# Reading one branch's result early and loading whole 128-partition tiles in the last two stages of a four-layer network

## The reference, cut to what matters

```python
ys = mamba_fwd(xs, spa_...)                     # over all pixels, 64 channels: the pixel mamba
ye = mamba_fwd(xe, spe_...)                     # over 8 tokens of each pixel's channels: the channel mamba
spa = silu(group_norm(ys, spa_gn_w, spa_gn_b, 4)) + x
spe = x + silu(group_norm(ye, spe_gn_w, spe_gn_b, 4))
w = softmax(att_w)
return spa * w[0] + spe * w[1] + x
```

## Time and profile before

| | us |
|---|---|
| median of three runs | 7533.4 |
| profiled execution, its own time | 7550.36 |
| span of that execution, first to last instruction | 7548.5 |
| channel mamba, first to last DMA issue | 5501.7 to 7320.2 |
| merge, first DMA issue to the end of the span | 7326.4 to 7548.5 |

### The profile page before, as it was taken

How to read it: one execution, slowest core, us unless ns; L and a number is a source line. 1 busy time by engine, 2 the same in 40 slices (tenths; PEclk the granted TensorE clock), 3 DMA queues, 4 the chain that set the end, 5 groups by cost and what they waited for, 6 DMA issues and landing times. The chain is left out here.

```text
span 7548.5 us, 120463 instructions
## 1 busy us (share of the span) xinstructions
PE 6575.4 (87%) x36560; PEld 3443.7 (46%) x36560; DVE 5590.7 (74%) x5630; ACT 3977.8 (53%) x6794; POOL 3832.4 (51%) x2716
## 2 busy tenths in 40 slices
PE   8968699999967379687999999999989999999970
PEld 7852233333345134574222222222257777777750
DVE  4653677777712278103999999999979999999974
ACT  4424466666612457103666666666655555555532
POOL 0100122222200300002888888888879999999960
PEclk9989799999978689757999999999989999999985
DMA  2243234334355523533222222222200000000016
GB/s 70 72 169 124 68 99 100 100 99 101 96 127 151 229 81 100 130 86 56 37 37 36 37 37 37 39 39 38 29 16 10 10 10 10 10 10 10 8 40 190
DMA packets 638233, 518.91 MB, mean 69 GB/s; under 512 B 249981, under 2 KB 569251, under 8 KB 629563
## 3 DMA queue, kind: packets, MB, share of 16 engines
q1 hardware_dynamic: 637947, 515.62, 27.9%
HBM read 304.91 MB, written 171.32 MB: 63 GB/s over the span
## 5 line engine op out<-in xcount | busy, mean ns | idle before, releaser
L2582 DVE TENSOR_TENSOR_SCAN spa_hs<-spa_p_d,spa_hs,spa_bx 128x483 f32<-128x483 f32 x1168 | 1370.3, 1223 | 21.1 <-ACT spa_p_d L2495 21.1
L2302 POOL TENSOR_TENSOR spa_hc<-spa_hs,spa_cr 128x966 f32<-128x966 f32 x592 | 1219.0, 2069 | 240.7 <-DVE spa_hs L2582 239.3
L2725 POOL TENSOR_TENSOR spe_hc<-spe_hs,spe_bcu 128x1024 f32<-128x1024 f32 x520 | 1219.7, 2362 | 64.5 <-DVE spe_hs L2937 63.5
L2937 DVE TENSOR_TENSOR_SCAN spe_hs<-spe_p_d,spe_bx 128x1024 f32<-128x1024 f32 x520 | 1161.4, 2275 | 35.0 <-ACT spe_p_d L2885 31.7
L2812 PEld LDWEIGHTS spe_p_y<-spe_idt,spe_hc 128*128 128x128 f32 x8320 | 965.1, 192 | 143.8 <-issue 143.8
L1065 DVE TENSOR_REDUCE attention_nm<-attention_p_s 128x2 f32<-128x640 f32 x1024 | 789.1, 812 | 260.2 <-PE attention_p_s L922 259.1
L2812 PE MATMUL spe_p_y<-spe_idt,spe_hc 128*128 128x128 f32 x8320 | 978.2, 276 | 0.0
L1023 ACT ACTIVATE attention_pr<-attention_p_t 128x512 f32<-128x512 f32 x1280 | 710.7, 599 | 420.3 <-PE attention_p_t L945 289.1
L2495 ACT ACTIVATE spa_p_d<-spa_p_d,spa_av 128x483 f32<-128x483 f32 x1184 | 703.9, 633 | 428.3 <-PE spa_p_d L2366 426.2
L2885 ACT ACTIVATE spe_p_d<-spe_p_d 128x896 f32<-128x896 f32 x520 | 445.5, 900 | 759.1 <-PE spe_p_d L2795 758.8
L2366 PE MATMUL spa_p_d<-spa_du,spa_hot 32*128 32x483 f32 x2368 | 657.0, 630 | 56.5 <-DVE spa_hs L2582 48.4
(11 more groups left out here) (425 smaller groups left out, 10630.8 us busy)
## 6 DMA issues: line engine op xcount, KB each, us to landing
attention_qs<-scratch_qp SPq DMA_DIRECT2D x768, 64.0 KB, 2.8
spa_uc<-spa_du SPq DMA_DIRECT2D x148, 241.5 KB
attention_rc<-scratch_den SPq DMA_DIRECT2D x128, 256.0 KB
scratch_qp<-patch_parts SPq DMA_DIRECT2D x64, 384.0 KB, 2.3
spa_xt<-scratch_x SPq DMA_DIRECT2D x148, 121.5 KB, 2.7
front_xs<-in_x_dram SPq DMA_DIRECT2D x64, 256.0 KB, 3.0
scratch_xf<-front_out SPq DMA_DIRECT2D x128, 128.0 KB, 2.5
patch_x<-scratch_xf SPq DMA_DIRECT2D x8, 2048.0 KB, 19.8
```

Of the source, the lines that this page charges most:

```text
L2302: nc.gpsimd.tensor_tensor(hc[:, k % 8:k % 8 + 2, :], hs[:, k:k + 2, :], cr2[:, s % 2, :].unsqueeze(1).broadcast_to([128, 2, NA]), ALU.mult ...
L2582: nc.vector.tensor_tensor_scan(hs[:, k, v], p_d[k % 4][:, v], bx[:, k, v], 0.0 if start else hs[:, k, NA - 1:NA], ALU.mult, ALU.add).then_ ...
L2725: nc.gpsimd.tensor_tensor(hc[:, k, :, d, :].rearrange("p s d t -> p d s t"), hs[:, k % 2, d, :, :], rows, ALU.mult)\
L2937: nc.vector.tensor_tensor_scan(hs[:, k % 2, d].rearrange("p d s t -> p (d s t)"), p_d[h][:, :], bx[:, k % 2, d].rearrange("p d s t -> p (d ...
```

## The change

- `by_batch` views a scratch tensor as [p, c, n] for each a: two images, 64 channels, columns. One DMA with this source fills 128 partitions. It serves the result of the pixel mamba, that of the channel mamba, and `x`.
- The pixel mamba's result goes into a tile `v_spa` that outlives the stages. SP issues its two loads at the start of the channel mamba, behind the first four loads of `spe_xt`.
- In the merge, `ye` comes in four DMAs of 128 partitions and 4160 columns; `bn_stats` takes half an image of `v_spa`, then the same half of `ye`.
- `x` has four tile buffers. One DMA of 128 partitions fills one, three tiles ahead of the tile that is stored.
- The constant columns are written once per output buffer and a (4 times in place of 16). The loops are written out instead of run on registers.

```diff
+def by_batch(t):
+    return t.rearrange("c (a p n) -> a p c n", a=2, p=2)
...
             for s in range(UE):
                 load(s, s)
+            for a in range(2):
+                sp.dma_start(v_spa[:, a, :], by_batch(ys)[a]).then_inc(spa_in, 16)
             stream(sp, NC, UE, HEAD, 4, (0, next_load), (3, store))
             for s in range(2):
                 sp.wait_ge(stored[s], 16 * ((NC + 1 - s) // 2))
+            sp.wait_ge(spa_in, 32)
...
-    NS = H // NR // 2
+    NS, UX = H // NR // 2, 4
...
-        v = [st.sb(f"v{q}", [128, 2, K]) for q in range(2)]
-        xs = st.sb("xs", [128, 2, N])
+        v = [v_spa, st.sb("v", [128, 2, K])]
+        xs = st.sb("xs", [128, UX, N])
...
-            for q, src in enumerate((ys, ye)):
-                for a in range(2):
-                    for p in range(2):
-                        sp.dma_start(v[q][64 * p:64 * p + 64, a, :], src[:, (2 * a + p) * K:(2 * a + p + 1) * K]).then_inc(v_in[2 * q + a], 16)
-            for a in range(2):
-                @turns(sp, NS)
-                def _(j):
-                    for s in range(2):
-
-                        sp.wait_ge(x_scaled[s], a * NS + j)
-                        for p in range(2):
-                            sp.dma_start(xs[64 * p:64 * p + 64, s, :], x2[:, bass.ds((2 * j + s) * N + (2 * a + p) * K, N)])\
-                                .then_inc(x_in[s], 16)
-                    for s in range(2):
-                        sp.wait_ge(merged[s], a * NS + j + 1)
-                        sp.wait_ge(filled[s], a * NS + j + 1)
-                        sp.dma_start(ov[:, a, bass.ds((2 * j + s) * NR, NR), :], os[:, s]).then_inc(stored[s], 16)
+            for i in range(4):
+                a, h = i // 2, i % 2
+                sp.dma_start(v[1][:, a, h * K // 2:(h + 1) * K // 2], by_batch(ye)[a][:, :, h * K // 2:(h + 1) * K // 2]).then_inc(v_in[i], 16)
+
+            def load(a, n, u):
+                sp.dma_start(xs[:, u, :], by_batch(x2)[a][:, :, n * N:(n + 1) * N]).then_inc(x_in[u], 16)
+
+            for i in range(UX):
+                load(0, i, i)
+            for i in range(4 * NS):
+                a, n, s = i // (2 * NS), i % (2 * NS), i % 2
+                if i + UX - 1 < 4 * NS and i:
+                    k = i + UX - 1
+                    sp.wait_ge(x_scaled[k % UX], k // UX)
+                    load(k // (2 * NS), k % (2 * NS), k % UX)
+                sp.wait_ge(merged[s], i // 2 + 1)
+                sp.wait_ge(filled, 2 * a + s + 1)
+                sp.dma_start(ov[:, a, n * NR:(n + 1) * NR, :], os[:, s]).then_inc(stored[s], 16)
...
+                if n < 2:
+
+                    if a:
+                        act.wait_ge(stored[s], 16 * NS)
+                    nc.scalar.activation(os[:, s, :, L:W - LR], zv[:, a:a + 1].unsqueeze(2).broadcast_to([128, NR, W - LR - L]),
+                                         ACT.Copy).then_inc(filled, 1)
...
+            half = K // BN // 2
             for i in range(4):
-                dve.wait_ge(v_in[i], 32)
...
+                for q in range(2):
+                    if q:
+                        dve.wait_ge(v_in[i], 16)
+                    for n in range(half * (i % 2), half * (i % 2) + half):
+                        nc.vector.bn_stats(bs[:, 2 * q + i // 2, n, :], v[q][:, i // 2, n * BN:(n + 1) * BN]).then_inc(counted, 1)
...
+                if i >= 2:
+                    dve.wait_ge(stored[s], 16 * (i // 2))
```

More of the change, by code:

```diff
@@ L2606, with spectral_mamba @@
 LF = B * H * FULL
-def spectral_mamba(nc, x2, w_in, w_conv, w_xd, w_dt, w_bc, dt_b, skip_d, a_wide, a_mask, w_out, ident, ye):
+def by_batch(t):
+    return t.rearrange("c (a p n) -> a p c n", a=2, p=2)
+def spectral_mamba(nc, x2, w_in, w_conv, w_xd, w_dt, w_bc, dt_b, skip_d, a_wide, a_mask, w_out, ident, ye, ys, v_spa):
     NC, UE, HEAD = LF // GP, 4, 9
@@ L2654, in spectral_mamba @@
             st.sem(n) for n in ("bc_done", "cu_copied", "bx_ready", "bx_pool", "summed", "y_ready", "out_done", "out_copied"))
+        spa_in = st.sem("spa_in")
         dta_done, decayed, scanned, weighted = st.sem2("dta_done"), st.sem2("decayed"), st.sem2("scanned"), st.sem2("weighted")
@@ L2954, with merge_branches @@
 BN = 416
-def merge_branches(nc, ys, ye, x2, gmat, gwb, att, out):
+def merge_branches(nc, v_spa, ye, x2, gmat, gwb, att, out):
     K = H * FULL
-    NS = H // NR // 2
+    NS, UX = H // NR // 2, 4
     N = NR * FULL
@@ L2989, in merge_branches @@
         v_in = [st.sem(f"v_in{i}") for i in range(4)]
-        x_in, filled, silu_ready, x_scaled, added, merged, stored = (st.sem2(n) for n in (
-            "x_in", "filled", "silu_ready", "x_scaled", "added", "merged", "stored"))
+        x_in, x_scaled = [st.sem(f"x_in{u}") for u in range(UX)], [st.sem(f"x_scaled{u}") for u in range(UX)]
+        filled = st.sem("filled")
+        silu_ready, added, merged, stored = (st.sem2(n) for n in ("silu_ready", "added", "merged", "stored"))
         ov = out.rearrange("(a p) c h w -> (p c) a h w", a=2)
@@ L3027, in _ @@
             act.wait_ge(const_ready, 1)
[L3028 to L3040, removed]
+            for i in range(4 * NS):
+                a, n, s = i // (2 * NS), i % (2 * NS), i % 2
+                if i >= 2:
+                    act.wait_ge(merged[s], i // 2)
+                for q, t in enumerate((t1, t2)):
+                    nc.scalar.activation(t[:, s, :], v[q][:, a, n * N:(n + 1) * N], ACT.Silu,
+                                         scale=sh[:, 0, q, a:a + 1], bias=sh[:, 1, q, a:a + 1]).then_inc(silu_ready[s], 1)
+                if n < 2:
[3 more added lines that the diff above has]
+                                         ACT.Copy).then_inc(filled, 1)
         @block.tensor
@@ L3099, in _ @@
             nc.vector.scalar_tensor_tensor(zv[:, :], zs[:, 1, :], at[:, 4:5], zv[:, :], ALU.mult, ALU.add).then_inc(const_ready, 1)
[L3100 to L3118, removed]
@@ new lines, in _ @@
+            for i in range(4 * NS):
+                a, n, s, u = i // (2 * NS), i % (2 * NS), i % 2, i % UX
+                dve.wait_ge(x_in[u], 16 * (i // UX) + 16)
+                if i:
+                    dve.wait_ge(merged[1 - s], (i + 1) // 2)
+                nc.vector.tensor_scalar(tx[:, :], xs[:, u, :], at[:, 6:7], None, ALU.mult).then_inc(x_scaled[u], 1)
+                dve.wait_ge(silu_ready[s], 2 * (i // 2) + 2)
+                dve.wait_ge(x_scaled[u], i // UX + 1)
+                nc.vector.scalar_tensor_tensor(tx[:, :], t1[:, s, :], at[:, 3:4], tx[:, :], ALU.mult, ALU.add).then_inc(added[s], 1)
+                dve.wait_ge(added[s], i // 2 + 1)
+                if i >= 2:
+                    dve.wait_ge(stored[s], 16 * (i // 2))
+                tv = tx[:, :].rearrange("p (r w) -> p r w", w=FULL)
+                sv = t2[:, s, :].rearrange("p (r w) -> p r w", w=FULL)
+                nc.vector.scalar_tensor_tensor(os[:, s, :, 0:L], sv[:, :, 0:L], at[:, 4:5], tv[:, :, 0:L], ALU.mult, ALU.add)
+                nc.vector.scalar_tensor_tensor(os[:, s, :, W - LR:W], sv[:, :, L:FULL], at[:, 4:5], tv[:, :, L:FULL], ALU.mult,
+                                               ALU.add).then_inc(merged[s], 1)
@@ L3387, in build @@
     nonzero = t["xf2"][:, SHIFT:SHIFT + LF]
-    spectral_mamba(nc, nonzero, *of("e_in e_conv e_xd e_dt e_bc e_dtb e_d e_alog decay_mask e_out ident ye"))
-    merge_branches(nc, t["ys"][:, SHIFT:SHIFT + LF], t["ye"], nonzero, *of("groups16 m_gn m_att"), out)
+    with nc.sbuf_tensor("v_spa", [128, 2, H * FULL], F32) as v_spa:
+        spectral_mamba(nc, nonzero, *of("e_in e_conv e_xd e_dt e_bc e_dtb e_d e_alog decay_mask e_out ident ye"),
+                       t["ys"][:, SHIFT:SHIFT + LF], v_spa)
+        merge_branches(nc, v_spa, t["ye"], nonzero, *of("groups16 m_gn m_att"), out)
 def kernel(**inputs):
```

## The result

The changed kernel takes 7748.9 us in the median of four runs (7741.5 to 7775.0), the kernel before 7542.4 in the same comparison (7525.0 to 7562.6). The ratio is 1.0283, with a 95% interval of 1.0254 to 1.0312: 206 us slower by the medians, 192 to 235 us by the interval. The forecast was 252 us slower, 7785 us, in a range of 7695 to 7870.

What follows compares the result with a forecast made beforehand. The prediction took the channel mamba as bound by TensorE and the merge by DMA. It added 86 us of channel mamba stall and restart and 166 us of merge, 252 us, to 7533.4, giving 7785 us, range 7695 to 7870.

Steps and rivals of the forecast that it cites:

- Two DMA engines by the source's first index: All new loads: the source's first index has two entries, so two of 16 DMA engines work, 51 GB/s together.
- Rate of an engine: New loads in both stages: each DMA engine moves 25.5 GB/s, with bounds of 12.9 and 25.9.
- D: Rival for the new loads: two engines at only 12.9 GB/s each, some 740 us more, 8275 us; chance 0.04.
- Later loads stand behind earlier ones: Channel mamba: the fifth chunk's load queues behind the two large loads, so TensorE waits 81 us.
- B: Rival: two engines but no channel mamba stall, small loads passing long ones; only the merge's 166 us, 7700; chance 0.06.
- Cold start, 5 us: Channel mamba after the stall: TensorE restarts at half clock, adding 5 us (0 to 10).
- Merge, 166 us: Merge: slower loads start the loop 78.4 us later and take 13.0 us a tile, ending 166 us later.
- Fills, written-out loops at 0: Merge loop: fewer constant fills and written-out loops bring or cost 0 (-2 to +4 us for the loops).
- Sum: Both changed stages: 86 us in the channel mamba plus 166 in the merge, 252 us slower.
- A: The forecast itself: two engines, later DMAs waiting behind them; 7785 us, own range 7750 to 7825; chance 0.80.
- C: Rival for the new loads: sixteen engines at 364 GB/s, no stall, 99 us less, 7434 us; chance 0.10.

Runs made afterwards that it cites:

- e4: Changed kernel with partition 2c + p, so each source has 64 channels first, then two images; 7441.7 us, 0.9870 of the kernel before.
- e5: Changed kernel with the two early loads issued from ScalarE's queue after the constants and first four chunks landed; 7698.9 us, 1.0205 of the kernel before.
- e6: Against e4, the constant columns are filled for each tile again; 7453.1 us, 0.9880 of the kernel before.
- e3: Changed kernel with all three kinds of load split into DMAs of 64 partitions; 7458.5 us, 0.9885 of the kernel before.
- e1: Changed kernel with the two early loads issued at the top of ScalarE's list, on its queue; 7783.5 us, 1.0326 of the kernel before.

## Why the prediction was right

- *Two DMA engines by the source's first index*: held. 0.13 and 0.14 of the engines; with 64 first 0.90 to 0.99 (e4). The rule of the Trainium skill that stood beside this step (DMA: Bandwidth & Descriptors, "Why a DMA increments its semaphore by 16 and not by 1") gives two as well, and sixteen for 64 and 128; both agree with these shares.
- *Rate of an engine*: taken as 25.5 GB/s, measured 26.6, just above the best row that I had (25.9). This is the term that was off. Both loads took about 160 us instead of 167, and a tile 12.6 us instead of 13.0, of which the rate alone gives 12.5. The lower bound, 12.9, is out, and with it D: a packet of 33 KB took 1.23 us in the early load, where D wanted 2.5.
- *Later loads stand behind earlier ones*: held. TensorE waited 74.9 us for 81. B is out: behind the large loads in the same queue the fifth chunk landed after 154.8 us; with them in another queue, and the constants already there, no chunk took more than 11.9 (e5).
- *Cold start, 5 us*: under 1 us. The clock was at 0.50 (1.2 GHz) and at 0.87 in the next 10 us, yet from the fifth chunk's `project_x` to the merge's first DMA it takes 1730.1 us, and before it took 1729.6. The stage grew by the wait alone. The clock did fall; why the slower matmuls cost so little isn't shown.
- *Merge, 166 us*: 147.1. The start of the loop was forecast 78 us later and came 71.3 later; the loop and end grew by 75.8 us. The sum had 88: 13.0 for 12.6 us a tile makes 6 of the difference. The other 6 lie in the 11 us that the sum put behind the sixteen tiles; from the last landing of `ye` (7540.0) to the end (7746.7) it is 16 x 12.6 us and 5 more.
- *Fills, written-out loops at 0*: held. The fills are 0.8 us by e6; the written-out loops were not tried alone, and in e3, which has them, no cost shows.
- *Sum*: 252 us forecast, 222 by stages, 206 by medians, with an interval (192 to 235) that holds 222. Of the 30 us between 252 and 222 about 19 follow from the engine's rate (6 in the wait, 7 before the loop, 6 in it), 5 are the cold start and 6 the loop's end. All of these errors point one way, so nothing cancelled: the mechanism carries the forecast, but the measured 7748.9 lies 1 us under A's own range (7750 to 7825), and inside the wider one.
- *Chance of C*: 0.10 was given to an outcome whose time was right for another kernel. The price was sound, the condition wasn't met: in e4 the loop starts 52 us earlier than before and is 46 us shorter, where C had 51 and 48.

## What to carry to other kernels

Before two DMAs are joined to one, look at the order of the indices on both sides: here a source that begins with two images got two DMA engines although it fills 128 partitions, and the same bytes with 64 channels first got all sixteen. A long DMA in front of a pipeline's small loads costs its whole duration less what the buffers cover; issue it from another queue, behind whatever the stage needs to begin, or make it fast. And a load moved under another stage is worth only what it was late by: 5 us here, once it was fast.

## What the runs showed of the hardware that I had not expected

- SP's own issue of a small DMA took 65.44 us behind the two large ones, and 38.9 us in the merge, where an issue otherwise takes 0.5. Before, behind 82 us of `merge_v` spread over sixteen engines, the longest issue of a load of `x` took 1.4 us. While an issue stands, SP's later waits and issues stand too. That the queue holds only so much is my reading; how much wasn't tried, nor what it costs.
- Two queues shared the busy DMA engines in turns of one packet (96 to 96 in 60 us of e1). A packet of 33 KB took 1.23 us there, so the small packets of the eleven constants, on the other queue, were 107 us in coming.
- Stores whose neighbouring partitions go to images 4 MB apart show no cost in e4: they land 6.2 us after their issue in the median, against 6.8 in e3.
